# The row minimum of the attention logits: four additions and one reduction in place of four additions with accumulators

## The chip, the cores and the metric

The kernel runs on one core of one Trainium2 chip. The core has four compute engines that work side by side: TensorE (PE: matmuls, with PEld for its weight loads), VectorE (DVE), ScalarE (ACT) and GpSimd (POOL). SyncE (SP) here only starts DMAs. Each engine works off its own list of instructions in order and waits at semaphores for the others. The metric is the time of one execution on the device in microseconds (us); lower is better.

## What is computed

There are 128 graphs of 128 nodes with 256 features each, and two layers. Cut to what matters:

```python
# layer 0: one aggregation with the adjacency matrix
h = jnp.maximum(_layernorm(x, axis=-1), 0.0)
x = x + adj @ (h @ W0) + b0
# layer 1: attention over the graph, 8 heads
h = jnp.maximum(_layernorm(x, axis=-1), 0.0)
feat_proj = (h @ fc_w + fc_b)            # split into 8 heads of 256
q = feat_proj @ q_w + q_b                # one number per node and head
k = feat_proj @ k_w + k_b
logits = q + jnp.swapaxes(k, -1, -2)
masked = logits + (1.0 - adj_mat[:, None]) * NEG
masked = jax.nn.leaky_relu(masked, negative_slope=0.01)
attn = jax.nn.softmax(masked, axis=-1)
out = attn @ feat_proj                   # heads joined, then @ fp_w + fp_b + h
x = x + jax.nn.sigmoid(out)
```

The change concerns the logits: a number per query is added to a row of masked keys, and the row's extreme value is wanted so that the exponentials stay in range. The kernel keeps the logits with reversed sign, so the extreme is a minimum.

## The kernel before

The graphs are taken in pairs: 64 pairs, pair p holding graphs j = 0 and 1. Nodes lie on the 128 partitions. The heads of a graph are taken in two chunks of four, c = 0 and 1, so a pair has four chunks (j, c). I call them A = (0,0), B = (0,1), C = (1,0) and D = (1,1). A chunk's logits are the tile `att[j][c]`, 128 partitions by 4 x 128 columns, and 4 further columns (CH to CH + 3) for the minima, one for each head.

The work on one chunk goes through the engines like this:

- `mask_keys` (POOL, L856) adds the key rows and the mask into `att`. It waits until PE has transposed the previous pair's `att` of the same chunk.
- `mask_min` (DVE, L563) adds the query of each head, a scalar for each partition, to its 128 columns in place, and takes the minimum through the accumulator.
- `leaky` (DVE, L570) works on all 516 columns: min(0.01 x, x), with `att` as both inputs.
- `exp` (ACT, L714) takes four exponentials with the minima as bias and sums them.
- `inverse` (DVE, L575) takes the reciprocal of the sums, and `normalise` (POOL, L863) multiplies the chunk by it.
- `transpose_p` (PE, L370) transposes the chunk into PSUM. `pT_high` (ACT, L721) and `pT_low` (DVE, L553) split it into a high and a low part, and `attend` (PE, ybank at L256) multiplies it with the projected features.

Beside it, PE projects the features (`project`, gbank at L256, eight per pair, numbers 0 to 7 through four PSUM banks); `g_high` (ACT, L707) and `g_low` (DVE, L546) read each bank and so free it. Layer 0 of later pairs runs in between: `aggregate` (PE, L323, three pairs ahead) reuses the bank that `residual0` (DVE, L524, writes `x`) reads, so it waits for that. `residual0` stands right behind `add_feats` (DVE, L582, writes `y`). Of later pairs, too, are `transpose_h` (PE, L341), `hT_high` (ACT, L688) and `hT_low` (DVE, L539), which free the way for `queries_keys` (PE, bank at L256). POOL also computes `xb` (L846), `t_pos` (L848), the features with bias (L872) and the last sum `res` (L879).

The order on each engine is written by hand: a function `step` per engine lists the calls for one pair. A loop of four pairs per turn (`pipeline`) runs it, so that a DVE turn comes every fourth pair. On DVE a step goes: hT_low, g_low 1, minima A, leaky A, minima B, pT_low of the previous pair's D, minima C, leaky B, inverse A, leaky C, g_low 0, minima D, g_low 5, g_low 2, leaky D, inverse B, add_feats, residual0, pT_low A, and the rest. On PE, `project` 7 takes the bank that g_low 2 frees, and `aggregate` follows it.

Of the kernel before, what the change touches and what calls it, by code (L numbers as in the profile page):

```python
# [7 lines left out]
ALU = mybir.AluOpType  # L8
# [6 lines left out]
J = 2  # L15
# [4 lines left out]
HC = 4  # L20
NC = H // HC
GC = H * D // BANK
CH = HC * P
# [12 lines left out]
def gnn_pair(nc, graph, identity, head_mask, row_coef, w0, bias0, fc_wT, fc_b, qk_w, q_b, k_b, fp_w, fp_b, out):  # L36
# [6 lines left out]
    with ExitStack() as ctx:  # L43
# [6 lines left out]
        def sem(name):  # L50
            return ctx.enter_context(nc.semaphore(name))

        def two(name, shape, dt=F32):

            return [sb(f"{name}{k}", shape, dt) for k in range(2)] * (U // 2)

        def sems(name, n):
            return [sem(f"{name}{k}") for k in range(n)]
# [41 lines left out]
        qs = two("qs", [P, J, H])  # L100
# [38 lines left out]
        a_h1, g_feats, pe_zT, a_hThi, v_hTlo = [sem(n) for n in ("a_h1", "g_feats", "pe_zT", "a_hThi", "v_hTlo")]  # L139
        pe_kq, a_kq, pe_kqT, a_qs = [sem(n) for n in ("pe_kq", "a_kq", "pe_kqT", "a_qs")]  # L140
        pe_g, a_g, v_g = sems("pe_g", J * GC), sems("a_g", J * GC), sems("v_g", J * NC)
        g_keys, v_mx, v_leaky = sems("g_keys", J * NC), sems("v_mx", J * NC), sems("v_leaky", J * NC)
        a_exp, v_rinv, g_norm = sems("a_exp", J * NC), sems("v_rinv", J * NC), sems("g_norm", J * NC)
        pe_pT, a_pT, v_pT = sems("pe_pT", J * NC), sems("a_pT", J * NC), sems("v_pT", J * NC)
# [284 lines left out]
        def _(dve):  # L429
# [126 lines left out]
            def mask_min(p, q, j, c):  # L556

                a = att[j][c]
                dve.wait_ge(g_keys[NC * j + c], p + 1)
                dve.wait_ge(a_qs, p + 1)  # L560
                for h in range(HC):
                    s = slice(h * P, (h + 1) * P)
                    r = dve.tensor_scalar(a[:, s], a[:, s], qs[q][:, j, c * HC + h:c * HC + h + 1], None, ALU.add,  # L563
                                          ALU.min, accum_out=a[:, CH + h:CH + h + 1])
                r.then_inc(v_mx[NC * j + c], 1)

            def leaky(p, j, c):
                a = att[j][c]
# [15 lines left out]
            def step(i, q):  # L584
                if later(i + 1):
                    hT_low(i + 1, (q + 1) % U)
                if has(i):
                    g_low(i, 1)
                    mask_min(i, q, 0, 0)
                    leaky(i, 0, 0)  # L590
                    mask_min(i, q, 0, 1)
                if has(i - 1):
                    pT_low(i - 1, 1, 1)
                if has(i):
                    mask_min(i, q, 1, 0)
                    leaky(i, 0, 1)
                    inverse(i, 0, 0)
                    leaky(i, 1, 0)
                    g_low(i, 0)
                    mask_min(i, q, 1, 1)  # L600
                    g_low(i, 5)
                    g_low(i, 2)
                    leaky(i, 1, 1)
                    inverse(i, 0, 1)
# [366 lines left out]
```

## Time and profile before

| | |
|---|---|
| median of three runs | 1509.34 us (1508.4 to 1509.9) |
| the profiled execution | 1508.82 us, of which the span from the first to the last instruction is 1507.0 |
| mean granted TensorE clock | 0.987 |
| PE busy | 1463.6 us (97%) |
| DVE busy | 1249.0 us (83%), 4267 instructions |
| POOL busy | 1079.1 us (72%) |
| ACT busy | 1078.9 us (72%) |

The table is one execution's. An engine's busy share is a mean over the whole span; what one engine's delay costs is seen only from who waits for it. PE's granted clock has two levels, 1.2 and 2.4 GHz, and the number is the share of the higher one. Instructions of one engine overlap a little: the next may start before the former has ended, so durations add up to more than the distance of their starts.

### The profile page before, as it was taken

Reading aid. Unit: us, or ns where it says so; the run is one execution under the profiler, and the core shown is the slowest. Engines: PE = TensorE matmul, PEld = TensorE weight load, DVE = VectorE, ACT = ScalarE, POOL = GpSimd, SP = SyncE. Lnnn points to the kernel's source line nnn. Section 1 sums busy time; section 2 is a strip of 40 time slices with the busy share of each in tenths; the row PEclk is TensorE's granted clock in tenths of the full one; section 3 lists DMA queues with packets and bytes.
Section 4 is the critical chain, followed back from the end, with each engine's and each line's share of the span. In section 5 each row is a group of like instructions: output and inputs, shape, how many; then the busy total and the mean of one; then the engine's idle time right before and its main releaser. Section 6 shows DMA issues by size and latency. Waiting matters only on the chain.

```text
span 1507.0 us, 32030 instructions
## 1 busy us (share of the span) xinstructions
PE 1463.6 (97%) x9640; PEld 1309.5 (87%) x9640; DVE 1249.0 (83%) x4267; ACT 1078.9 (72%) x3480; POOL 1079.1 (72%) x1292
## 2 busy tenths in 40 slices
PE   7999999999999999999999999999999999999998
PEld 6888998988988888888888888888888888888887
DVE  5888887878878798787887888878887888888886
ACT  3677777777767677676776767767777777777776
POOL 2677776777767777776876767767777677777765
PEclk8899999999999999999999999999999999999999
DMA  4222122122121221221221212212212112122211
GB/s 170 86 92 99 59 92 99 54 94 85 63 98 61 87 98 58 90 98 50 98 98 50 98 57 91 98 57 91 84 72 91 73 74 99 66 81 98 84 49 44
DMA packets 33410, 123.70 MB, mean 82 GB/s; under 512 B 4640, under 2 KB 8096, under 8 KB 25120
## 3 DMA queue, kind: packets, MB, share of 16 engines
q1 hardware_dynamic: 33024, 122.77, 21.5%
q14 instruction: 83, 0.68, 0.2%
q8 instruction: 15, 0.25, 0.1%
q10 hardware_dynamic: 288, 0.01, 0.0%
HBM read 105.46 MB, written 17.30 MB: 81 GB/s over the span
## 4 chain that ended last, share of the span: by engine, by line
PE 88%; issue 5%; ACT 3%; DVE 2%; POOL 1%; DMA 0%; DVEq 0%; POOLq 0%; SPq 0%; ACTq 0%
PE gbank L256 43%; PE ybank L256 22%; PE bank L256 9%; PE tbank L370 7%; PE bank L323 4%; PE bank L341 1%; ACT g_hi L707 1%; PE gbank L276 1%; ACT pT_hi L721 1%; ACT h L683 1%; DVE ah_lo L517 1%; DVE hT_lo L539 1%; PE bank L355 0%; DMA fp_sb<-fp_w_dram 0%; ACT ah_hi L678 0%
## 5 line engine op out<-in xcount | busy, mean ns | idle before, releaser
L856 POOL TENSOR_TENSOR att<-keys,t_pos 128x512 f32<-128x512 f32 x256 | 328.6, 1294 | 150.4 <-PE tbank L370 149.7
L256 PE MATMUL gbank<-m_hi,hT_lo 128*128 128x512 f32 x1024 | 427.9, 418 | 0.0
L256 PE MATMUL gbank<-m_lo,hT_hi 128*128 128x512 f32 x1024 | 405.5, 396 | 0.0
L256 PE MATMUL gbank<-m_hi,hT_hi 128*128 128x512 f32 x1024 | 404.6, 395 | 0.0
L714 ACT ACTIVATE att<-att 128x128 f32<-128x128 f32 x1024 | 396.5, 395 | 2.0 <-DVE att L570 2.0
L863 POOL TENSOR_TENSOR att<-att,rinv 128x512 f32<-128x512 f32 x256 | 289.5, 1131 | 143.9 <-DVE rinv L575 142.1
L721 ACT ACTIVATE pT_hi<-tbank 128x512 fp32r<-128x512 f32 x256 | 153.4, 599 | 285.5 <-PE tbank L370 285.5
L546 DVE TENSOR_TENSOR g_lo<-gbank,g_hi 128x512 fp32r<-128x512 f32 x512 | 336.6, 678 | 24.6 <-ACT g_hi L707 22.2
L707 ACT ACTIVATE g_hi<-gbank 128x512 fp32r<-128x512 f32 x512 | 289.7, 595 | 43.9 <-PE gbank L256 43.9
L256 PE MATMUL ybank<-g_hi,pT_lo 128*128 128x256 f32 x1024 | 301.2, 294 | 0.0
L563 DVE TENSOR_SCALAR_CACHE_REDUCE att<-att,qs 128x128 f32<-128x128 f32 x1024 | 291.1, 340 | 0.0
L256 PE MATMUL ybank<-g_lo,pT_hi 128*128 128x256 f32 x1024 | 290.6, 284 | 0.0
L256 PE MATMUL ybank<-g_hi,pT_hi 128*128 128x256 f32 x1024 | 290.5, 284 | 0.0
L553 DVE TENSOR_TENSOR pT_lo<-tbank,pT_hi 128x512 fp32r<-128x512 f32 x256 | 176.4, 689 | 92.9 <-ACT pT_hi L721 85.0
L256 PEld LDWEIGHTS gbank<-m_hi,hT_hi 128*128 128x128 f32 x1024 | 194.0, 189 | 46.2
L256 PEld LDWEIGHTS gbank<-m_hi,hT_lo 128*128 128x128 f32 x1024 | 194.2, 190 | 29.0 <-DVE g_lo L546 0.3
L256 PEld LDWEIGHTS gbank<-m_lo,hT_hi 128*128 128x128 f32 x1024 | 194.3, 190 | 27.5
L256 PEld LDWEIGHTS ybank<-g_hi,pT_lo 128*128 128x128 f32 x1024 | 197.3, 193 | 6.0 <-DVE pT_lo L553 0.2
L256 PEld LDWEIGHTS ybank<-g_lo,pT_hi 128*128 128x128 f32 x1024 | 197.0, 192 | 5.5
L714 ACT ACTIVATION_READ_ACCUMULATOR att<-att 128x1 f32 x1024 | 198.5, 194 | 0.0
L256 PEld LDWEIGHTS ybank<-g_hi,pT_hi 128*128 128x128 f32 x1024 | 196.6, 192 | 0.0
L570 DVE SCALAR_TENSOR_TENSOR att<-att 128x516 f32<-128x516 f32 x256 | 189.4, 740 | 2.2
(89 smaller groups left out, 2433.2 us busy)
## 6 DMA issues: line engine op xcount, KB each, us to landing
keys<-key_rows SPq DMA_DIRECT2D x64, 1024.0 KB, 5.3
g_in<-graph_dram SPq DMA_DIRECT2D x64, 512.0 KB, 3.3
out_dram<-res SPq DMA_DIRECT2D x64, 256.0 KB, 2.0
fp_sb<-fp_w_dram SPq DMA_DIRECT2D x4, 512.0 KB, 9.2
att<-fc_wT_dram SPq DMA_DIRECT2D x2, 512.0 KB, 6.5
feats<-fc_wT_dram SPq DMA_DIRECT2D x2, 512.0 KB, 9.9
key_rows<-kq_sb SPq DMA_DIRECT2D x64, 8.0 KB, 1.3
w_f<-w_dram SPq DMA_DIRECT2D x1, 256.0 KB, 8.3
```

The costliest lines, as they stand in the source:

```text
L256: mm = pe.matmul(out_ap, w, m, start=first and n == 0, stop=last and n == len(terms) - 1)
L323: mm = pe.matmul(sums[:, j, dt, :], h0_f[q][:, j, dt * P:(dt + 1) * P], adjT_of(q)[:, j, :], start=True, stop=True)
L370: mm = pe.transpose(tbank[:, h * P:(h + 1) * P], att[j][c][:, h * P:(h + 1) * P], ident[:])
L546: dve.tensor_tensor(g_lo[j][:, s], bank[:], g_hi[j][:, s].bitcast(F32), ALU.subtract)\
L553: dve.tensor_tensor(pT_lo[j][:, hs, :], rows, pT_hi[j][:, hs, :].bitcast(F32), ALU.subtract)\
L563: r = dve.tensor_scalar(a[:, s], a[:, s], qs[q][:, j, c * HC + h:c * HC + h + 1], None, ALU.add, ALU.min, accum_out=a[:, CH + h:CH + h + 1])
L570: dve.scalar_tensor_tensor(out=a, in0=a, scalar=SLOPE, in1=a, op0=ALU.mult, op1=ALU.min)\
L707: act.activation(g_hi[j][:, s], gbank[tenant(RING, RSIZE, n, p)[0]][:], ACT.Copy).then_inc(a_g[n], 1)
L714: e = act.activation(a[:, s], a[:, s], ACT.Exp, scale=-1.0, bias=a[:, CH + h:CH + h + 1], accum_out=esum[j][c][:, h:h + 1])
L721: act.activation(pT_hi[j][:, c * HC:(c + 1) * HC, :], rows, ACT.Copy).then_inc(a_pT[NC * j + c], 1)
L856: gp.tensor_tensor(a, keys[q][:, j, c * HC:(c + 1) * HC, :], t_pos[q][:, j, :].unsqueeze(1).broadcast_to([P, HC, P]), ALU.add)\
L863: gp.tensor_tensor(a, a, rinv[j][c][:].unsqueeze(2).broadcast_to([P, HC, P]), ALU.mult)\
```

## The change

`mask_min` loses the accumulators. The four additions of a chunk (one for each head, 128 columns, in place, the scalar from memory) stay as plain additions. The last of them raises a new semaphore, `v_add`, one for each chunk; DVE waits for it, and a new instruction reads the 4 x 128 columns and writes the four minima, `tensor_reduce` along the innermost axis. It raises `v_mx`, which `leaky` waits for as before. Nothing else changes, on no other engine.

```diff
@@ -139,6 +139,7 @@
         pe_g, a_g, v_g = sems("pe_g", J * GC), sems("a_g", J * GC), sems("v_g", J * NC)
+        v_add = sems("v_add", J * NC)
         g_keys, v_mx, v_leaky = sems("g_keys", J * NC), sems("v_mx", J * NC), sems("v_leaky", J * NC)
@@ -560,9 +561,11 @@
                 for h in range(HC):
                     s = slice(h * P, (h + 1) * P)
-                    r = dve.tensor_scalar(a[:, s], a[:, s], qs[q][:, j, c * HC + h:c * HC + h + 1], None, ALU.add,
-                                          ALU.min, accum_out=a[:, CH + h:CH + h + 1])
-                r.then_inc(v_mx[NC * j + c], 1)
+                    r = dve.tensor_scalar(a[:, s], a[:, s], qs[q][:, j, c * HC + h:c * HC + h + 1], None, ALU.add)
+                r.then_inc(v_add[NC * j + c], 1)
+                dve.wait_ge(v_add[NC * j + c], p + 1)
+                dve.tensor_reduce(a[:, CH:CH + HC], a[:, 0:CH].rearrange("p (h n) -> p h n", h=HC),
+                                  mybir.AxisListType.X, ALU.min).then_inc(v_mx[NC * j + c], 1)
```

DVE's list before, the minima of chunks B and C. `g_keys` and `a_qs` are the semaphores of POOL's masked keys and ACT's queries, `v_mx` that of the minima, numbered 0 to 3 for A to D:

```order
L563 TENSOR_SCALAR att<-att,qs 128x128 [waits a_qs,g_keys1]
L563 TENSOR_SCALAR att<-att,qs 128x128 x3
L553 TENSOR_TENSOR pT_lo<-tbank,pT_hi 128x512 [waits a_pT3]
L563 TENSOR_SCALAR att<-att,qs 128x128 [waits a_qs,g_keys2]
L563 TENSOR_SCALAR att<-att,qs 128x128 x3
L570 SCALAR_TENSOR_TENSOR att<-att 128x516 [waits v_mx1]
```

The same piece of DVE's list now, chunks B and C:

```order
L564 TENSOR_SCALAR att<-att,qs 128x128 [waits a_qs,g_keys1]
L564 TENSOR_SCALAR att<-att,qs 128x128 x3
L567 TENSOR_REDUCE att<-att 128x4 [waits v_add1]
L554 TENSOR_TENSOR pT_lo<-tbank,pT_hi 128x512 [waits a_pT3]
L564 TENSOR_SCALAR att<-att,qs 128x128 [waits a_qs,g_keys2]
L564 TENSOR_SCALAR att<-att,qs 128x128 x3
L567 TENSOR_REDUCE att<-att 128x4 [waits v_add2]
L573 SCALAR_TENSOR_TENSOR att<-att 128x516 [waits v_mx1]
```

Nothing has moved against anything else. One instruction with a wait on DVE's own additions stands between them and whatever followed them.

## Rows read from the trace of the kernel before

**Rows 1.** The page's fourth part: the chain that ended last, by engine.

```profile
PE 88%; issue 5%; ACT 3%; DVE 2%; POOL 1%; DMA 0%; DVEq 0%; POOLq 0%; SPq 0%; ACTq 0%
```

**Rows 2.** The waits of the whole span: us in total, times, longest.

```profile
PE bank L256 <- DVE hT_lo L539: 26.6, 12, 2.4
```

**Rows 3.** The chain in order of time, 780 to 850: start us, us, what.

```profile
825.13 0.72 PE bank L256 x12
...
838.10 0.89 PE bank L323 x8
...
847.37 0.72 PE bank L256 x12
```

**Rows 4.** DVE's timeline, one pair: start us, us, line, what, idle time before.

```profile
823.00 0.69 DVE L539 TENSOR_TENSOR hT_lo<-bank,hT_hi 128x512 fp32r<-128x512 f32 x1 [0.45 <-ACT hT_hi L688]
...
824.21 0.34 DVE L563 TENSOR_SCALAR_CACHE_REDUCE att<-att,qs 128x128 f32<-128x128 f32 x1
...
825.39 0.70 DVE L570 SCALAR_TENSOR_TENSOR att<-att 128x516 f32<-128x516 f32 x1
826.00 0.34 DVE L563 TENSOR_SCALAR_CACHE_REDUCE att<-att,qs 128x128 f32<-128x128 f32 x1
...
827.07 0.69 DVE L553 TENSOR_TENSOR pT_lo<-tbank,pT_hi 128x512 fp32r<-128x512 f32 x1
...
831.33 0.34 DVE L563 TENSOR_SCALAR_CACHE_REDUCE att<-att,qs 128x128 f32<-128x128 f32 x1
```

**Rows 5.** Busy time of DVE alone in one stretch: us, busy (instructions).

```profile
823.00:836.20 13.20, 12.28 (x46) 1.00 0.12 40
```

**Rows 6.** Groups of DVE instructions by line and shape: busy us, mean ns.

```profile
L546 DVE TENSOR_TENSOR g_lo<-gbank,g_hi 128x512 fp32r<-128x512 f32 x512 | 336.6, 678 | 24.6 <-ACT g_hi L707 22.2
...
L444 DVE SCALAR_TENSOR_TENSOR c_part<-fp_sb,fcb,c_part 128x256 f32<-128x256 f32 x15 | 7.1, 472 | 0.0
L433 DVE TENSOR_TENSOR m_lo<-gbank,m_hi 128x258 fp32r<-128x258 f32 x16 | 6.6, 414 | 3.2 <-ACT m_hi L640 3.1
...
L441 DVE TENSOR_SCALAR c_part<-fp_sb,fcb 128x256 f32<-128x256 f32 x1 | 0.4, 353 | 0.6 <-DMA fp_sb<-fp_w_dram 0.6
```

**Rows 7.** Single lines: duration in ns, minimum, median, maximum.

```profile
L563 DVE TENSOR_SCALAR_CACHE_REDUCE att<-att,qs x1024: 327/341/352, 48.4 to 1487.2; 128x128 f32<-128x128 f32 x171
...
L570 DVE SCALAR_TENSOR_TENSOR att<-att x256: 654/686/1742, 49.6 to 1488.6; 128x516 f32<-128x516 f32 x128
```

**Rows 8.** POOL's timeline of the same pair.

```profile
823.41 1.29 POOL L856 TENSOR_TENSOR att<-keys,t_pos 128x512 f32<-128x512 f32 x1
826.46 1.30 POOL L856 TENSOR_TENSOR att<-keys,t_pos 128x512 f32<-128x512 f32 x1 [1.77 <-PE tbank L370]
827.72 1.30 POOL L879 TENSOR_TENSOR res<-sg,x 128x512 f32<-128x512 f32 x1
830.25 1.40 POOL L863 TENSOR_TENSOR att<-att,rinv 128x512 f32<-128x512 f32 x1 [1.24 <-DVE rinv L575]
831.62 1.28 POOL L846 TENSOR_TENSOR xb<-g_in,b_row 128x512 f32<-128x512 f32 x1
832.99 1.07 POOL L848 TENSOR_SCALAR t_pos<-g_in 128x256 f32<-128x256 f32 x1
834.84 1.04 POOL L863 TENSOR_TENSOR att<-att,rinv 128x512 f32<-128x512 f32 x1 [0.78 <-DVE rinv L575]
```

**Rows 9.** DVE's timeline at another place, leaky behind a turn.

```profile
342.86 1.74 DVE L570 SCALAR_TENSOR_TENSOR att<-att 128x516 f32<-128x516 f32 x1
```

**Rows 10.** POOL's timeline at that place.

```profile
342.75 1.29 POOL L856 TENSOR_TENSOR att<-keys,t_pos 128x512 f32<-128x512 f32 x1 [4.26 <-PE tbank L370]
344.01 1.76 POOL L879 TENSOR_TENSOR res<-sg,x 128x512 f32<-128x512 f32 x1
```

**Rows 11.** PE behind two turns: us, busy (matmuls), granted clock, DMA.

```profile
801.13:804.13 3.00, 2.96 (x20) 0.51 0.00 0
893.95:896.95 3.00, 2.96 (x30) 1.00 0.00 0
```

## The prediction

> **What bounds the kernel now.** Read first the chain that ended last [rows 1]: PE carries 88% of it, DVE 2%. DVE is not the bound, but it feeds PE at many points. The waits of the whole span [rows 2] show one place where PE stands for DVE: the matmuls of queries and keys wait for hT_lo 12 times, 26.6 us in all, once per turn of the loop over four pairs. Inside the turns PE has no gap. So the question is how much later DVE may get before PE feels it. One undisturbed pair answers it. From the chain [rows 3], one pair takes 847.37 - 825.13 = 22.24 us, and the aggregate of the pair three ahead starts at 838.10. I count t from the start of hT_lo at 823.00 [rows 4]. DVE starts the four minima at t = 1.21 (chunk A), 3.00 (B), 4.67 (C, not shown; pT_lo at 4.07 takes 0.60) and 8.33 (D), and residual0 (x, L524) ends at 13.20, the end of the stretch of [rows 5]. The aggregate reuses residual0's bank and starts at t = 15.10. So that step has 1.90 us of slack, and up to it DVE was busy 12.28 of 13.20 us, which gives 0.92 us of idle time ahead of it. Together 2.82 us per pair: DVE work added by the minima costs nothing up to that, and beyond it PE waits one for one. Behind the aggregate, DVE's waits hang on PE again, so the same delay comes in every pair.
>
> **The price of the instructions.** Removed per chunk: four additions with accumulator. They stand 1.07 us in all (826.00 to 827.07, [rows 4]), so 0.267 each, and one lasts 341 ns [rows 7]. Added: four additions without. No row has them at 128 columns. The nearest is L441, 128x256 with a scalar from memory, both operands in SBUF: 353 ns, against 472 ns for L444, which has the same columns and a second stream [rows 6]. Of DVE's single rate L546 and L433 tell: 512 columns in 678 ns, 258 in 414, so 1.04 ns a column. 256 columns at that rate take 266 ns, and the 119 ns that L441 is shorter are close to half of it. So the plain addition moves columns at double rate, and 128 columns save 67 ns: 275 ns long, 0.20 us apart. Bounds: 0.14 us apart if some 60 ns of accumulator reading go too, 0.267 if nothing is gained. The reduction reads 512 columns in one stream; the nearest row is leaky's 516: 0.61 us from 825.39 to 826.00, 0.69 long. It must wait for the last addition's end; for the wait itself I add 0.03, an estimate from leaky, which starts 0.11 us after the four additions' slots are over (825.39 against 824.21 + 1.07) and waits for the same thing. A chunk then holds DVE for 3 x 0.20 + 0.275 + 0.03 + 0.61 = 1.51 us in place of 1.07: +0.44, or +1.76 us per pair (bounds +0.27 and +0.71 a chunk, +1.1 and +2.8 a pair). Queued behind the new wait on DVE are pT_lo for B, leaky for A, and g_lo for D; they wait that long. By this alone DVE stays within 2.82 us, and the change costs nothing. Neither bound is a gain: the reduction alone takes 0.57 of the 1.07 us that is freed. POOL, ACT, SP and PE get no instruction more or less.
>
> **The collision.** POOL's instructions are long: 1.29 us for L856, L879 and L846, 1.07 for L848, 1.04 for L863 when nothing holds it [rows 8]. Where leaky, which reads two streams from SBUF, meets one, it stands still. At 342.86 it took 1.74 us instead of the median of 0.69 [rows 7, 9]; L856 had started on POOL at 342.75 and ended at 344.04 [rows 10]. So leaky was held 1.05 us, until 343.91. The next POOL instruction, started at 344.01 without a gap, took 1.76 instead of 1.30: it was held until about 344.47, when leaky was nearly through. Two facts follow: a holder keeps the path for its whole instruction, and the one that waits gets it next, even between two POOL instructions that stand back to back. The additions with accumulator are never held: 327 to 352 ns over all 1024 of them, whatever POOL does [rows 7] (one stream at single rate). The new additions fetch one tensor at double rate, which needs the second path that leaky uses for its second input. So I take it that they collide, and each of the four on its own. The Trainium skill says the same (SBUF — State Buffer, Who interferes with whom): tensor_scalar in a 2-port mode, not the form that writes its accumulator, locks the port pair shared with GpSimd, and the second to come is blocked fully. Without that rule being true of the new additions the sum would be 1509 us; with it, what follows. The trace agrees as far as leaky goes and cannot show the additions.
>
> **One pair, walked through**, from [rows 4, 8], with an addition holding the path about 0.13 us and leaky 0.56. Chunk A: L856 on POOL (823.41) keeps the first addition from t = 1.21 to 1.57; reduction 2.47, leaky 3.19, next 3.80. L856 for chunk D asks at 3.46, gets the path at 3.75, keeps it to 4.91. Chunk B: its first addition starts at 4.91; POOL's next, L879, is waiting by then, takes over at 5.05 for 1.16 us; the second addition asked at 5.11, too late, and starts at 6.21. Reduction 6.91, next at 7.52 instead of 4.07. Chunk C meets nothing: 8.12 to 9.63. Leaky B, inverse, leaky C and g_lo bring us to 11.54. L863 asks when the inverse is done, gets the path when leaky C is through (10.89) and keeps it to 11.8. Chunk D: one addition at 11.8, then L846 until 13.05, the second addition, then L848 until about 14.25, then the rest; reduction 14.75, next at 15.35 instead of 9.40. Two g_lo end at 16.6, leaky D, the inverse, add_feats and residual0 end at 18.58. The aggregate starts at 18.6 instead of 15.10: **3.5 us a pair**. PE also stands earlier in it, from about 13.8 until the second g_lo is done at 16.6, since project 7 needs that bank: 2.8 us in one piece, and the rest ahead of the aggregate. What is late next is PE itself, with everything behind it.
>
> **The clock.** The idle times at the turns, up to 2.4 us [rows 2], were followed in 6 of 12 by about 3 us at half clock (1.2 GHz, granted 0.50 to 0.54), in the other 6 by full clock [rows 11]. In three us at half clock PE does half the work, so 1.5 us are lost. A new idle time of 2.8 us per pair can do the same; about 0.6 of the 1.5 falls into PE's second wait, so 1.0 a pair where it happens. I take it in half of the pairs, as at the turns: 0.5.
>
> **Sum.** 62 of 64 pairs run like this (the first and last run with PE waiting anyway): 62 x (3.5 + 0.5) = 248 us. The profiled span is 1507.0; the median lies 2.3 above it. 1507.0 + 248 + 2.3 = 1757 us. At the turns DVE's stall of 4 us gives little more, and I leave it out.
>
> **Rivals.** (1) No collision: the additions run at single or double rate on a path of DVE's own. DVE gets 1.1 to 2.8 us a pair more, within the 2.82, and PE never waits: 1509 us, not slower. It decides at one question, whether a plain addition that meets a POOL instruction is longer than 275 to 341 ns. For it: nothing shows such an addition being held. Against: leaky is, and L441's rate. (2) The four additions keep the path between them, once they have it, because they stand only 0.20 us apart. Then chunk B loses 1.1 us once and D 0.26 once; residual0 ends at 15.5, the aggregate slips 0.4: 62 x 0.4 + some 5 us at the turns = 1540 us. For it: no two DVE instructions that need the path stand together in the trace. Against: the holder's share is shorter than the spacing, and POOL took over at once at 344.47. Between (2) and the forecast lie mixtures, where one of the three POOL instructions is passed (each is 1.1 to 1.3 us a pair, 70 to 80 us). (3) The clock falls in every pair: 62 x 4.5 = 279, 1788 us; with nothing of the 1.5 us absorbed, 62 x 5.0 = 310, 1819. (4) The change does less DVE work: the lower bounds, 0.14 and 0.57, still make 1.34 a chunk against 1.07. I see no way to faster but a better phase at the turns, where PE has 26.6 us to win.
>
> **Chances.** Forecast with full alternation, at either clock, 55% (1700 to 1825); mixtures and (2) 28% (1535 to 1700); no collision 13%; faster by a way I don't see 3%; above 1830 1%. The range of 1535 to 1830 holds about 83%. A measurement of this kernel can tell about 0.2%. Slower by more than that 84%, within it 12%, faster 4%.
>
> **What would show it.** Additions: their mean at L564 near 275 ns if free, 500 ns or more if held, with single ones of 1.1 to 1.5 us in chunks B and D; near 340 refutes the double rate. The reduction near 690 ns, never held. POOL's groups a little longer (L863 and L846). PE waits inside every pair, for g_lo (ring bank of project 7) and for x ahead of the aggregate, and a period of 25.7 to 26.7 us; the mean granted clock below 0.987. If DVE's busy time grows by only 1.8 us a pair and the period stays at 22.24, rival (1) holds. If four additions run together behind one block, rival (2) does. I am wrong in size if the order in which the path is granted differs, or if a POOL instruction lets additions through.

## The result, and the profile after

The changed kernel takes 1665.79 us (median of 4 runs, 1664.83 to 1666.03) against 1508.87 us in the same comparison: a ratio of 1.104, 95% interval 1.1021 to 1.106. That is slower by 157 us; the forecast was 248 us. The time lies within the range of 1535 to 1830 us, but below the 1700 to 1825 that the prediction gave to full alternation (55%); it lies in the stretch of the mixtures (28%).

The page of the changed kernel first, its busy times and its chain by engine:

```profile
PE 1497.4 (90%) x9640; PEld 1291.3 (78%) x9640; DVE 1564.6 (94%) x3499; ACT 1096.8 (66%) x3480; POOL 1100.8 (66%) x1292
...
DVE 54%; PE 25%; issue 15%; ACT 4%; POOL 0%; DMA 0%; DVEq 0%; POOLq 0%; SPq 0%; ACTq 0%
```

DVE has become the engine that sets the time: 54% of the chain where [rows 1] had 2%. It executes 768 instructions fewer and is busy 316 us longer. These are its groups by line (busy us, mean ns), the new addition, leaky and the reduction, and the durations of the first and the last in single (minimum/median/maximum):

```profile
L564 DVE TENSOR_SCALAR att<-att,qs 128x128 f32<-128x128 f32 x1024 | 422.2, 473 | 0.0
...
L573 DVE SCALAR_TENSOR_TENSOR att<-att 128x516 f32<-128x516 f32 x256 | 237.8, 929 | 2.2
L567 DVE TENSOR_REDUCE att<-att 128x4 f32<-128x512 f32 x256 | 175.7, 686 | 8.8
```

```profile
L564 DVE TENSOR_SCALAR att<-att,qs x1024: 271/279/1405, 48.4 to 1645.0; 128x128 f32<-128x128 f32 x171
...
L567 DVE TENSOR_REDUCE att<-att x256: 685/686/689, 51.5 to 1645.3; 128x4 f32<-128x512 f32 x128
```

An addition with nothing in its way takes 279 ns; the mean of 473 comes from single ones of up to 1405. The reduction never varies. Now one pair on DVE, the counterpart of [rows 4]; four additions stand in one row:

```profile
803.30 0.69 DVE L540 TENSOR_TENSOR hT_lo<-bank,hT_hi 128x512 fp32r<-128x512 f32 x1 [0.45 <-ACT hT_hi L691]
...
804.51 1.63 DVE L564 TENSOR_SCALAR att<-att,qs 128x128 f32<-128x128 f32 x4
806.17 0.69 DVE L567 TENSOR_REDUCE att<-att 128x4 f32<-128x512 f32 x1
806.89 1.71 DVE L573 SCALAR_TENSOR_TENSOR att<-att 128x516 f32<-128x516 f32 x1
808.53 1.92 DVE L564 TENSOR_SCALAR att<-att,qs 128x128 f32<-128x128 f32 x4
...
811.08 0.68 DVE L554 TENSOR_TENSOR pT_lo<-tbank,pT_hi 128x512 fp32r<-128x512 f32 x1
811.67 0.87 DVE L564 TENSOR_SCALAR att<-att,qs 128x128 f32<-128x128 f32 x4
...
813.18 0.69 DVE L573 SCALAR_TENSOR_TENSOR att<-att 128x516 f32<-128x516 f32 x1
...
815.05 2.24 DVE L564 TENSOR_SCALAR att<-att,qs 128x128 f32<-128x128 f32 x4
817.33 0.69 DVE L567 TENSOR_REDUCE att<-att 128x4 f32<-128x512 f32 x1
817.93 1.28 DVE L547 TENSOR_TENSOR g_lo<-gbank,g_hi 128x512 fp32r<-128x512 f32 x2
...
820.40 0.68 DVE L525 TENSOR_TENSOR x<-bank,xb 128x512 f32<-128x512 f32 x1
...
828.62 0.69 DVE L540 TENSOR_TENSOR hT_lo<-bank,hT_hi 128x512 fp32r<-128x512 f32 x1 [0.46 <-ACT hT_hi L691]
```

The pair takes 828.62 - 803.30 = 25.32 us instead of 22.24. Chunk C, which meets no POOL instruction, goes from 811.67 to 813.18: 1.51 us. Chunks A, B and D are longer, and so is the leaky of A. POOL beside it, the counterpart of [rows 8]:

```profile
804.17 1.30 POOL L859 TENSOR_TENSOR att<-keys,t_pos 128x512 f32<-128x512 f32 x1
806.75 1.30 POOL L859 TENSOR_TENSOR att<-keys,t_pos 128x512 f32<-128x512 f32 x1 [1.28 <-PE tbank L371]
808.01 1.76 POOL L882 TENSOR_TENSOR res<-sg,x 128x512 f32<-128x512 f32 x1
814.03 1.40 POOL L866 TENSOR_TENSOR att<-att,rinv 128x512 f32<-128x512 f32 x1 [4.26 <-DVE rinv L578]
815.40 1.28 POOL L849 TENSOR_TENSOR xb<-g_in,b_row 128x512 f32<-128x512 f32 x1
816.77 1.13 POOL L851 TENSOR_SCALAR t_pos<-g_in 128x256 f32<-128x256 f32 x1
```

And single additions, the first of chunk B, and the first, second and fourth of chunk D:

```profile
808.53 1.33 DVE L564 TENSOR_SCALAR att<-att,qs 128x128 f32<-128x128 f32 x1
```

```profile
815.05 0.47 DVE L564 TENSOR_SCALAR att<-att,qs 128x128 f32<-128x128 f32 x1
...
815.44 1.32 DVE L564 TENSOR_SCALAR att<-att,qs 128x128 f32<-128x128 f32 x1
...
816.88 0.41 DVE L564 TENSOR_SCALAR att<-att,qs 128x128 f32<-128x128 f32 x1
```

In B, res stands in POOL's list right behind L859. L859 held leaky A (1.71 us instead of 0.69), leaky A held res (1.76 instead of 1.30), and res held B's first addition. In D the first addition waited 0.2 us for normalise, then xb got its turn and held the second 1.05 us. PE's waits in that pair, in its timeline:

```profile
815.49 0.66 PE L371 MATMUL tbank<-ident,att 128*128 128x128 f32 x4 [0.34 <-POOL att L866]
819.27 0.50 PE L257 MATMUL gbank<-m_hi,hT_lo 128*128 128x512 f32 x1 [1.71 <-DVE g_lo L547]
821.22 1.02 PE L324 MATMUL bank<-g_in,h_f 128*128 128x128 f32 x7 [0.28 <-DVE x L525]
```

Two of them stand where the prediction put them: in front of project 7 for g_low 2, and in front of the aggregate for x. The first, in front of transpose A for POOL's normalise, it did not have. One more thing was not foreseen. The waits of the whole span have no longer any "issue" ahead of hT_lo; the 12 turns of the loop, where PE waited 26.6 us in all [rows 2], have become pairs like the others.

### The profile page after: what moved, and what is told of

Same layout as the page of the kernel before. It is cut to its first block, busy times and chain, and to the rows that moved or that the text cites. A ratio compares the mean times of both kernels' runs of the same rounds, so it can differ in the third digit from the quotient of the medians.

```text
span 1664.2 us, 31262 instructions
## 1 busy us (share of the span) xinstructions
PE 1497.4 (90%) x9640; PEld 1291.3 (78%) x9640; DVE 1564.6 (94%) x3499; ACT 1096.8 (66%) x3480; POOL 1100.8 (66%) x1292
## 4 chain that ended last, share of the span: by engine, by line
DVE 54%; PE 25%; issue 15%; ACT 4%; POOL 0%; DMA 0%; DVEq 0%; POOLq 0%; SPq 0%; ACTq 0%
DVE att L564 25%; PE gbank L257 11%; DVE att L567 8%; DVE g_lo L547 8%; PE ybank L257 5%; DVE att L573 5%; PE bank L324 4%; PE tbank L371 3%; DVE pT_lo L554 3%; ACT hT_hi L691 2%; DVE x L525 2%; DVE y L585 2%; ACT g_hi L710 2%; DVE rinv L578 1%; PE gbank L277 1%
## 5 line engine op out<-in xcount | busy, mean ns | idle before, releaser
L257 PE MATMUL gbank<-m_hi,hT_lo 128*128 128x512 f32 x1024 | 434.0, 424 | 106.9 <-DVE g_lo L547 106.9
L564 DVE TENSOR_SCALAR att<-att,qs 128x128 f32<-128x128 f32 x1024 | 422.2, 473 | 0.0
L859 POOL TENSOR_TENSOR att<-keys,t_pos 128x512 f32<-128x512 f32 x256 | 329.3, 1299 | 86.3 <-PE tbank L371 85.4
L547 DVE TENSOR_TENSOR g_lo<-gbank,g_hi 128x512 fp32r<-128x512 f32 x512 | 330.8, 677 | 1.1 <-ACT g_hi L710 0.9
L573 DVE SCALAR_TENSOR_TENSOR att<-att 128x516 f32<-128x516 f32 x256 | 237.8, 929 | 2.2
L717 ACT ACTIVATION_READ_ACCUMULATOR att<-att 128x1 f32 x1024 | 192.5, 188 | 0.0
```

The source lines that it names most:

```text
L257: mm = pe.matmul(out_ap, w, m, start=first and n == 0, stop=last and n == len(terms) - 1)
L547: dve.tensor_tensor(g_lo[j][:, s], bank[:], g_hi[j][:, s].bitcast(F32), ALU.subtract)\
L573: dve.scalar_tensor_tensor(out=a, in0=a, scalar=SLOPE, in1=a, op0=ALU.mult, op1=ALU.min)\
L717: e = act.activation(a[:, s], a[:, s], ACT.Exp, scale=-1.0, bias=a[:, CH + h:CH + h + 1], accum_out=esum[j][c][:, h:h + 1])
L859: gp.tensor_tensor(a, keys[q][:, j, c * HC:(c + 1) * HC, :], t_pos[q][:, j, :].unsqueeze(1).broadcast_to([P, HC, P]), ALU.add)\
```

## Experiments

All times are medians, the ratio is to the kernel before in the same comparison. Each starts from one of the two kernels.

**Where the stall at the turns comes from.** The kernel before, with 56 small memsets ahead of DVE's loop:

```diff
+                for n in range(56):
+                    dve.memset(spare[:, n:n + 1], 0.0)
                 dve.wait_ge(pe_crow, 1)
```

> The kernel before, with 56 memsets of one column ahead of DVE's loop; nothing else differs. It asks where the stall of 3.9 to 4.2 us on DVE at each of 12 turns of the loop comes from, which the changed kernel no longer shows. Theory F-place: DVE's instructions are fetched in blocks, and the loop's list (240 instructions of the program and 64 accumulator reads) straddles one block more than fits; moved by 56 instructions it does not, the stall is gone, and with it 12 x 3.2 us of PE's time: 1470 to 1475 us, hT_lo at a turn waits for ACT. Rival F-length: the list's length alone decides: the stall stays, 1509 to 1513 us.

1469.81 us, ratio 0.9744 (0.9728 to 0.976): 38.5 us faster than before, with nothing but 56 idle instructions more. Every pair takes 22.24 us, the turns too. The row of the waits on hT_lo and the row of the instruction queue (packets, MB); the kernel before had 83 packets, 0.68 MB in that queue:

```profile
DVE hT_lo L542 <- ACT hT_hi L691: 30.7, 64, 2.1
```

```profile
q14 instruction: 23, 0.19, 0.0%
```

So 60 packets of instructions, five at each of 12 turns, are no longer fetched.

**Is it the length of the list?** The changed kernel, with the loop's list as long as before:

```diff
+                if not isinstance(i, int):
+                    for n in range(12):
+                        dve.memset(spare[:, n:n + 1], 0.0)
```

> The changed kernel with 12 memsets of one column per pair at the end of DVE's step, inside the loop only, so that the loop's list is as long as before (304) and starts where it did. The memsets take 0.06 us each, 0.7 us a pair, of which DVE's wait for hT_hi (0.45 us) hides a part. Theory F (place or length): the stall at the turn is back, 12 x 3.6 us: 1666 + 43 + 12 to 35 = 1720 to 1745 us. Rival: the stall went because DVE is the bound and does not wait there: no stall, 1675 to 1705 us.

1665.32 us, ratio 1.104 (1.1021 to 1.1058): as the changed kernel, no stall, and the memsets cost nothing either. Neither alternative held. Length alone is not it. I had miscounted the start: the changed kernel has 80 accumulator reads fewer ahead of the loop and 20 reductions more, so this loop starts 60 instructions earlier than before. With length and start as before:

> The run with the longer loop (changed kernel, 304 instructions in the loop's list) had no stall at the turns. I had counted 20 accumulator reads ahead of the loop where there are 80: the kernel before has 60 more instructions there than the changed one, so the two loops start at different places. This kernel puts 60 memsets ahead of the loop, so that length and start are both as in the kernel before. Theory F-place: the stall of some 4 us is back at 12 turns, 12 x 3.6 = 43 us and up to 4 for the memsets: 1705 to 1715 us. Rival (the changed kernel is free of it for another reason): 1665 to 1670 us.

1713.38 us, ratio 1.1365 (1.1346 to 1.1384): the stall is back, and with it 48 us. Its waits:

```profile
DVE hT_lo L543 <- issue: 61.7, 12, 5.4
```

```profile
q14 instruction: 82, 0.67, 0.1%
```

**The size of a block.** The kernel before with the same memsets, 256 and 24 of them:

> The kernel before with 256 memsets of one column ahead of DVE's loop. If the instructions are fetched in blocks of 256, the loop lies in its blocks as in the kernel before, and the stall at the turns stays: 1508 plus up to 15 us for the memsets (0.06 each), 1509 to 1524. Rival (any shift cures it, or the block has another size): 1470 to 1485 us.

> The kernel before with 24 memsets ahead of DVE's loop. From the runs so far (blocks of 256, a window of two blocks): the loop of 304 must start more than 208 instructions into a block before, and 236 to 255 from the run with the second reduction, which has no stall at 40 more and a length of 336. Then 24 more put the start at the front of the next block: no stall, 1469 to 1471 us. Rival (the start lies elsewhere): 1508 to 1511 us.

256: 1512.67 us, ratio 1.0033 (1.0021 to 1.0044), the stall is there (48.5 us over 12 turns, 85 packets). 24: 1470.08 us, ratio 0.9747 (0.9731 to 0.9763), no stall. Moving the list by 256 restores what moving by 24 or 56 cures. So what counts is where the list lies in blocks whose size divides 256, and how long it is. The Trainium skill names the size (Runtime: NRT & Kernel Launch, Instruction fetch mechanics): instructions come in blocks of 256 into a store of two, and a branch back to one that has left it waits for a fetch. All runs here agree with that, but they don't single it out: blocks of 128 in a store of three would give the same pattern of stalls. With the skill's size, an estimate: the loop of the kernel before starts 236 to 255 instructions into a block. The 236 comes from the run with one reduction below (20 more ahead of the loop, 320 in it, no stall), and not from the one with two, as the expectation of the 24 memsets has it; that one gives 216. A list of 304 then touches three blocks; moved by 24 it starts in the next one and touches two.

**The reduction without the collision.** The kernel before, accumulating additions kept, with wait and reduction behind:

```diff
-                r.then_inc(v_mx[NC * j + c], 1)
+                r.then_inc(v_add[NC * j + c], 1)
+                dve.wait_ge(v_add[NC * j + c], p + 1)
+                dve.tensor_reduce(a[:, CH:CH + HC], a[:, 0:CH].rearrange("p (h n) -> p h n", h=HC),
+                                  mybir.AxisListType.X, ALU.min).then_inc(v_mx[NC * j + c], 1)
```

> The kernel before with its accumulating additions, and behind them the wait and the reduction of the changed kernel. So DVE gets the new reduction without the new form of addition. Slack theory: 0.64 to 0.75 us a chunk, 2.6 to 3.0 a pair, about the 2.82 us that DVE has: 1507 to 1525 us (or up to 39 less, if the stall at the turn goes since the list has moved), additions at 341 ns and never held. Rival (the reduction and its wait are what costs, not the collision): most of the 157 us, 1600 us or more.

1476.5 us, ratio 0.9788 (0.9771 to 0.9804). The list moved by 20, the stall is gone, so the run to compare with is the shifted one of 1469.81: the reduction alone costs 6.7 us. The period stays at 22.23 us, although DVE has 2.24 us more to do up to the end of residual0, 14.52 us in place of the 12.28 of [rows 5] (the stretch in us, then DVE's busy time):

```profile
802.39:817.08 14.69, 14.52 (x51) 1.00 0.10 33
```

Additions as before:

```profile
L565 DVE TENSOR_SCALAR_CACHE_REDUCE att<-att,qs 128x128 f32<-128x128 f32 x1024 | 291.4, 341 | 0.0
L575 DVE SCALAR_TENSOR_TENSOR att<-att 128x516 f32<-128x516 f32 x256 | 175.9, 687 | 2.2
```

**Twice the reduction.** The same with a second reduction of each chunk, into spare columns.

> As the run with accumulating additions and one reduction, with a second reduction per chunk into spare columns: 5.0 to 5.4 us of DVE work a pair over the kernel before, and no collision. Slack theory: 5.2 - 2.82 = 2.4 us a pair, 62 x 2.4 = 149: 1620 to 1680 us, and PE waits in each pair for g_lo and for x, as in the changed kernel. Rival (DVE's work is hidden, only collisions cost): below 1530 us.

1684.91 us, ratio 1.1171 (1.1153 to 1.119), a period of 25.50 us: 3.26 us over 22.24, where the model said 2.4. From hT_lo to the end of residual0 DVE is busy 17.79 us, 5.51 over the 12.28. Some 0.9 of it is a hold of leaky A, whose row has a mean of 907 ns again, though nothing about leaky was changed: leaky A now starts late enough to meet POOL's addition of keys and mask for chunk D, as in the changed kernel. The other 4.6 us are plain work. So plain work on DVE, with no new form of addition, delays PE as the change does once it exceeds the slack. That 3.26 us come of 5.51 and not 2.7 is the slack, which is smaller than 2.82 (see below).

```profile
L577 DVE SCALAR_TENSOR_TENSOR att<-att 128x516 f32<-128x516 f32 x256 | 232.2, 907 | 2.2
```

**The collision without the reduction.** The changed kernel without reduction and wait. The minima are left out, and the mask's factor is 1. Cut to what matters; beside it POOL sets the four columns for chunk D's minima once, ahead of the loop:

```diff
-NEG = 1.0e9
+NEG = 1.0
...
-                r.then_inc(v_add[NC * j + c], 1)
-                dve.wait_ge(v_add[NC * j + c], p + 1)
-                dve.tensor_reduce(a[:, CH:CH + HC], a[:, 0:CH].rearrange("p (h n) -> p h n", h=HC),
-                                  mybir.AxisListType.X, ALU.min).then_inc(v_mx[NC * j + c], 1)
+                r.then_inc(v_mx[NC * j + c], 1)
```

> The changed kernel without the reduction and its wait: the minima are left out, and the mask's factor is 1 in place of 1e9 so that no row overflows. DVE has the plain additions and their collisions alone: 4 x 0.64 = 2.6 us a pair less than the changed kernel. Slack theory: the pair's period falls from 25.3 to about 22.7 us, 1490 to 1530 us. Rival (the collisions alone cost the 157 us, the reduction is hidden): 1620 us or more.

1471.88 us, ratio 0.976 (0.9742 to 0.9778), 2 us over the shifted kernel, and below the expected range, since with a period of 22.24 nothing was left of the 0.5 us a pair. The additions are held as long as in the changed kernel, and PE does not feel it:

```profile
L565 DVE TENSOR_SCALAR att<-att,qs 128x128 f32<-128x128 f32 x1024 | 423.3, 474 | 0.0
L571 DVE SCALAR_TENSOR_TENSOR att<-att 128x516 f32<-128x516 f32 x256 | 174.1, 680 | 2.2
```

So the reduction alone costs 7 us, the held additions alone 2 us, and both together 196 us (1665.79 - 1469.81). In busy time of DVE per pair: 1.97, 1.44 and 4.95 us over the shifted kernel. The last is 1.54 more than the sum of the first two; 1.14 of it is leaky. Its busy time is 184.9 us in the shifted kernel, where res holds leaky B for a moment in 61 pairs, 175.9 and 174.1 with one of the two, and 237.8 with both, where L859 holds leaky A in 60 of the pairs.

This run also shows something of POOL's `t_pos` (here L850). One addition starts 0.40 us after it and ends 0.40 us before it, at its free length; the same holds in 62 pairs:

```profile
811.58 1.08 POOL L850 TENSOR_SCALAR t_pos<-g_in 128x256 f32<-128x256 f32 x1
```

```profile
811.98 0.28 DVE L565 TENSOR_SCALAR att<-att,qs 128x128 f32<-128x128 f32 x1
```

**Moving POOL's instructions.** The changed kernel with `inputs` (xb and t_pos) ahead of normalise A in POOL's step:

```diff
-                if has(i):
-                    normalise(i, 0, 0)
                 if later(i + 2):
                     inputs(i + 2, (q + 2) % U)
                 if has(i):
+                    normalise(i, 0, 0)
+                if has(i):
                     normalise(i, 0, 1)
```

> The changed kernel with two POOL instructions, xb and t_pos, moved ahead of normalise A; so they run while DVE is at chunk B's reduction and chunk C, and no longer at chunk D. In the changed kernel D's additions and reduction hold DVE for 2.88 us, C's for 1.51. Collision theory: D falls to 1.5 to 1.8, C rises by 0 to 0.9 us; 0.3 to 1.3 us a pair, 1585 to 1645 us. Rival (the long additions in D are not POOL's doing, or cost nothing further down): 1660 to 1670 us.

1665.54 us, ratio 1.1044 (1.1023 to 1.1064): no gain; the rival's number, but not for the rival's reason. The four additions of chunk B, C and D in its timeline:

```profile
808.37 3.11 DVE L564 TENSOR_SCALAR att<-att,qs 128x128 f32<-128x128 f32 x4
...
812.72 0.86 DVE L564 TENSOR_SCALAR att<-att,qs 128x128 f32<-128x128 f32 x4
...
816.09 1.05 DVE L564 TENSOR_SCALAR att<-att,qs 128x128 f32<-128x128 f32 x4
```

D fell from 2.24 to 1.05 us, as collision predicts. But xb now stood right behind res, so B's first addition was held by res and another by xb: 3.11 instead of 1.92. That is the alternation that the prediction had for chunk B, close to the walk's 3.08 (3.80 to 6.88, the reduction's 6.91 less the 0.03 of its wait). What one chunk gave the other took: the additions' sum stayed at 420.4 us (422.2). I had expected POOL to reach xb later.

**One addition in place of four**, 128x512 with the query broadcast:

```diff
-                for h in range(HC):
-                    s = slice(h * P, (h + 1) * P)
-                    r = dve.tensor_scalar(a[:, s], a[:, s], qs[q][:, j, c * HC + h:c * HC + h + 1], None, ALU.add)
+                rows = a[:, 0:CH].rearrange("p (h n) -> p h n", h=HC)
+                r = dve.tensor_tensor(rows, rows,
+                                      qs[q][:, j, c * HC:(c + 1) * HC].unsqueeze(2).broadcast_to([P, HC, P]), ALU.add)
```

> The changed kernel with one addition per chunk of 128x512 (the query broadcast along its 128 columns) in place of four, then the same reduction. It reads two streams, as leaky does, so it can be held, but once. DVE gets 0.26 us a chunk, 1.05 a pair, over the kernel before, and holds of 1 to 2.5 us a pair; the loop's list is short (208), so no stall at the turns. Collision and slack theory: 1470 to 1525 us. Rival (a hold costs the same however many instructions there are): 1600 us or more.

1513.8 us (8 runs, 1506.5 to 1521.16), ratio 1.003 (1.0005 to 1.0054). Within the expected range, and a gain of 152 us on the changed kernel; against the shifted kernel it is 44 us slower. Its period changes from pair to pair, mostly 22.2 to 22.5 or 23.7 us: it sits at the edge of the slack, where a hold more or less decides, and the runs spread wider than of any other kernel. In the profiled run, the slowest of the eight, the 28 pairs of 23.7 us are those in which leaky A meets L859 and res behind it. The change takes plain work off DVE too, not only the number of holds, so this run doesn't separate the two.

The fastest kernel is the one before with its list moved (1469.81 with 56, 1470.08 us with 24 memsets). It beats both.

## Why the prediction was right, and where it was off

**The direction and the mechanism held.** POOL's instructions hold the plain additions (up to 1405 ns for one of 279), each on its own, and a holder is followed by the one that waits. The accumulating ones are held in no run (352 ns at most). Rival (1), no collision, is refuted by the rows. Rival (2), one hold for four additions, holds in B (where nothing stood behind res), but in chunk D, and in B of the run with moved POOL instructions, two holds followed each other.

**The prices of the instructions** were right: additions 279 ns for 275, the reduction 686 for 690, chunk C 1.51 us for 1.51.

**The slack** was there, but smaller than 2.82 us: the runs give 2.24. In the changed kernel DVE is busy 17.60 us from hT_lo to the end of residual0, 5.32 over the 12.28 of [rows 5], and the period grew by 3.08, so 2.24 cost nothing. With one reduction and accumulating additions DVE has just these 2.24 us more, and the period stays at 22.23. Beyond it PE waits one for one, as predicted: 5.51 us more give 3.26. The missing 0.58 is made up of four parts. The prediction took the aggregate's start, 838.10, from the chain, where a piece starts when the one before has ended; in the timeline it starts at 837.94 (0.16):

```profile
837.94 0.83 PE L323 MATMUL bank<-g_in,h_f 128*128 128x128 f32 x6
```

DVE keeps 0.18 us of its idle time even when it is late (17.78 - 17.60). The aggregate starts 0.14 us after the end of x, not at once. And from there to the next hT_lo it takes 7.40 us where it took 7.31 (837.94 to 845.25); why, no run tells.

**The walk** gave 18.58 us for the stretch that took 17.78. It is off in two places, and they partly cancel. The four additions of D were to take three holds; the last one, by t_pos (L851), came to 0.13 us instead of 1.0: chunk D took 2.88 us, not 3.81. The third addition started just ahead of t_pos, and the fourth, started 0.11 us behind it, ended 0.6 us before t_pos did (816.88 + 0.41 against 816.77 + 1.13). So the step "a holder keeps the path for its whole instruction", read from tensor_tensor alone, does not hold for this tensor_scalar: it lets additions through, which the prediction had named as a way to be wrong in size. The run without the reduction shows an addition in its middle that isn't held at all. And in chunk A, POOL's L859 stood 0.46 us later than in the old phase (at t = 0.87 instead of 0.41), so the first addition lost 0.76 us rather than 0.36, leaky A came behind L859 rather than ahead of it, and B lost one hold to it. A, leaky A and B together: 7.78 us for 7.52. With 3.5 a pair forecast and 3.08 measured, this term was 217 us where the runs give 196. That it came so close is partly luck: the walk was 0.80 us too long, and the point from which PE waits was put 0.40 too late (t = 15.10 instead of 14.70).

**The clock** term, 31 us, did not come: PE's longest wait in a pair was 1.71 us, not 2.8, and the granted clock is 0.994, above the 0.987 of before. In the changed kernel it stays at the higher level from 46 us after the start of the span to its last few us. Whether a wait of 2.8 us would have lowered it, the run doesn't tell.

**The signs.** The mean addition was 473 ns where 500 or more were named, the period 25.3 us instead of 25.7 to 26.7, and the clock rose instead of falling; the waits for g_lo and x and the reduction's 686 ns came as named. All three misses follow from the terms above.

**The turns** are the term whose sign was missed: "At the turns DVE's stall of 4 us gives little more, and I leave it out." I took the stall as given. It hangs on the number of instructions in and ahead of DVE's loop, which this change alters (304 to 256 in the loop), and it went away, for 38.5 us. DVE's wait for hT_lo at the turns had "issue" as its releaser in the trace, and I didn't ask what that was. The forecast was 91 us too high: 21 by the holds, 31 by the clock, 38.5 by the turns. All three err to the same side, and it is the width of the range that held the number. That 196 - 38.5 gives the measured 157 is no proof of its own, since both are taken against the shifted kernel. Without the lucky layout the changed kernel would be 205 us slower (1713.38 us, measured with 12 and 60 memsets in it).

## What to carry to other kernels

Before splitting an accumulating instruction in two, look at what the parts share with other engines: here the part that got faster (279 ns for 341) became one that GpSimd can hold for a microsecond. Count a helper engine's slack to the next deadline of the bound engine, and expect two harmless loads (2 and 7 us) to be harmful together (196 us). When every turn of a loop shows microseconds of "issue" on an engine, count the instructions in and ahead of it: 24 idle ones gained 2.5% here.

## What the runs showed of the hardware

- GpSimd's tensor_scalar t_pos (128x256, 1.08 to 1.13 us) holds a plain addition of VectorE only near its own start: one that started 0.11 us behind it lost 0.13 us, one that started 0.40 us behind it nothing (62 times). The tensor_tensor ones of 128x512 held an addition until they ended, by 1.05 us where it came right at their start and by 1.13 at most. Why t_pos differs, no run here tells.
- VectorE's tensor_reduce was never held: 685 to 690 ns in the changed kernel and in all runs with one reduction per chunk.
- A VectorE loop of 304 instructions stalls 3.9 to 5.4 us at each turn, with five packets of fetching, or not at all, by where its list lies: 256 memsets ahead of it leave the stall as it is, 24 remove it.
- Of the 12 turns of the kernel before, half were followed by 3 us at half clock [rows 11]; moved by 24 or 56 instructions, with the stall gone, the same kernel has a granted clock of 0.993 to 0.996 over the whole span.
